# Two attention stages of an eight-stage kernel: TensorE's wait for PSUM banks, taken per score tile instead of per pair of tiles

## What is computed

```python
x = x + _L0_attn_ref(_layernorm(x), ...)   # 16 heads of 16, keys at most 128 tokens away
x = x + _L0_ffn_ref(_layernorm(x), ...)    # 8 experts, 2 chosen for each token, and a shared one
x = x + _L1_attn_ref(_layernorm(x), ...)   # 16 heads of 16, blocks of 64: neighbours, first and last block
x = x + _L1_ffn_ref(_layernorm(x), ...)    # one linear layer with weights of -1, 0 and 1
```

## Time and profile before

| | us |
|---|---|
| median of 3 runs | 2714.09 (2711.36 to 2715.87) |
| the profiled execution | 2722.96 |
| its span, first to last instruction | 2721.2 |
| TensorE busy | 2236.0 (82% of the span) |
| VectorE busy | 1889.8 (69%) |
| ScalarE busy | 1691.1 (62%) |
| GpSimd busy | 1072.8 (39%) |

### The profile page before, as it was taken

How to read it: one execution, slowest core, us unless ns; L and a number is a source line. 1 busy time by engine, 2 the same in 40 slices (tenths; PEclk the granted TensorE clock), 3 DMA queues, 4 the chain that set the end, 5 groups by cost and what they waited for, 6 DMA issues and landing times. The chain is left out here.

```text
span 2721.2 us, 71969 instructions
## 1 busy us (share of the span) xinstructions
PE 2236.0 (82%) x25421; PEld 1285.8 (47%) x25421; DVE 1889.8 (69%) x5617; ACT 1691.1 (62%) x3876; POOL 1072.8 (39%) x1325
## 2 busy tenths in 40 slices
PE   7957888888877588859999994992999999998464
PEld 4622333333324376748888883551343434343243
DVE  4538888888826577644545455765999999996285
ACT  6935777777762355514545444770788888889243
POOL 3523444444447677746666662540000000000165
PEclk9977999999988799979999997995899999999687
DMA  7442222222203266645554344763122222221296
GB/s 231 182 145 57 75 75 80 77 76 74 80 21 123 68 164 187 168 127 118 135 129 102 91 89 133 256 228 106 45 74 70 75 69 75 70 74 35 62 180 152
DMA packets 393755, 297.94 MB, mean 109 GB/s; under 512 B 258592, under 2 KB 326944, under 8 KB 393408
## 3 DMA queue, kind: packets, MB, share of 16 engines
q1 hardware_dynamic: 375904, 249.02, 34.6%
q0 software_dynamic: 12960, 35.60, 3.8%
q10 hardware_dynamic: 4544, 8.72, 1.1%
HBM read 133.53 MB, written 123.69 MB: 95 GB/s over the span
## 5 line engine op out<-in xcount | busy, mean ns | idle before, releaser
L701 ACT ACTIVATE a_pr<-a_pst 128x384 f32<-128x384 f32 (+3 forms) x2176 | 934.5, 482 | 226.4 <-PE a_pst L736 189.1
L649 DVE TENSOR_REDUCE a_mx<-a_psc 128x1 f32<-128x384 f32 (+2 forms) x1152 | 587.9, 566 | 45.3 <-PE a_psc L736 35.6
L802 PE MATMUL a_po<-a_pr,a_ve 128*17 128x128 f32 (+3 forms) x10496 | 565.3, 303 | 2.2 <-ACT a_pr L701 1.3
L644 DVE CUSTOM_DVE_ANT_0 a_cut<-a_psc,row_mask 128x384 bf16<-128x384 f32 (+1 forms) x1024 | 497.3, 522 | 88.3 <-PE a_psc L736 41.7
L736 PE MATMUL a_psc<-a_ke,a_qe 52*128 52x128 f16 (+5 forms) x3072 | 375.4, 289 | 154.3 <-DVE a_mx L644 53.5
L623 POOL TENSOR_SCALAR_AFFINE_SELECT a_pr<-a_pr 128x512 f32<-128x512 f32 x448 | 275.0, 634 | 366.7 <-ACT a_pr L701 366.7
L736 PE MATMUL a_pst<-a_qe,a_ke 53*128 53x128 f16 (+5 forms) x3072 | 368.1, 284 | 41.6 <-ACT a_pr L701 19.8
L736 PEld LDWEIGHTS a_psc<-a_ke,a_qe 52*128 52x128 f16 (+1 forms) x3072 | 123.6, 94 | 351.1 <-DVE a_mx L644 187.4
L736 PEld LDWEIGHTS a_pst<-a_qe,a_ke 53*128 53x128 f16 (+1 forms) x3072 | 113.7, 94 | 356.7 <-ACT a_pr L701 323.5
L802 PEld LDWEIGHTS a_po<-a_pr,a_ve 128*17 128x17 f32 x10496 | 194.1, 96 | 185.6 <-issue 130.5
L861 POOL MEMSET t_spread<- 128x2048 f32 x1 | 1.8, 1804 | 706.6 <-POOLq L464 706.6
(11 more groups left out here) (233 smaller groups left out, 4264.2 us busy)
## 6 DMA issues: line engine op xcount, KB each, us to landing
a_qe<-qx SPq DMA_DIRECT2D x384, 64.0 KB, 2.8
a_ke<-kx SPq DMA_DIRECT2D x384, 64.0 KB, 2.8
vx<-p_vst SPq DMA_DIRECT2D x32, 544.0 KB, 3.2
a_ve<-vx SPq DMA_DIRECT2D x64, 272.0 KB, 3.2
ox<-a_ost SPq DMA_DIRECT2D x256, 68.0 KB
qx<-p_stg SPq DMA_DIRECT2D x64, 256.0 KB, 2.8
kx<-p_stg SPq DMA_DIRECT2D x64, 256.0 KB, 3.1
x_res<-x SPq DMA_DIRECT2D x16, 512.0 KB, 9.9
```

The source lines that it names most:

```text
L644: dve.tensor_tensor_reduce(out=cut[:, n % 4, 0:width], in0=psc[(u * n_s + n) % RING][:, 0:width], in1=row_mask[:, at:at + width], scale=1. ...
L649: dve.tensor_reduce(out.unsqueeze(1), psc[(u * n_s + n) % RING][:, 0:width], AXX, ALU.max)\
L701: act.activation(pr[s % SLOTS][:, h // 2, h % 2, 0:width], pst[prob_slot(u, n) % RING][:, 0:width], ACT.Exp, scale=scale).then_inc(p_ready, 1)
L802: last = pe.matmul(po[h][32 * a:32 * a + VW, tok % CH:tok % CH + w], ve[g][:, t, a * VW:(a + 1) * VW], pr[s % SLOTS][:, a // 2, a % 2, col ...
```

## The change

Each pass of a pair now waits head by head. The matmuls of the even head wait for their own bank, and the matmuls of the odd head for theirs. The helper `products`, which interleaved the two heads piece by piece, becomes `product`, which issues all pieces of one head and then counts `ready` up. So in jobs with two pieces the order of the four matmuls changes from (head 0, piece 0), (head 1, piece 0), (head 0, piece 1), (head 1, piece 1) to (head 0, piece 0), (head 0, piece 1), (head 1, piece 0), (head 1, piece 1). Nothing else is changed: rings, jobs, the order of pairs and the other engines' programs stay.

```diff
-            def products(outs, stats, movs, pieces, ready):
+            def product(par, out, stat, mov, pieces, ready):
 
                 for k, (tok, count, col) in enumerate(pieces):
-                    for par in range(2):
-                        last = pe.matmul(outs[par][:, col:col + count], stats[par], movs[par](tok, count),
-                                         start=(k == 0), stop=(k == len(pieces) - 1),
-                                         skip_group_check=True, tile_position=(64 * par, 0))
-                        if k == len(pieces) - 1:
-                            last.then_inc(ready, 1)
+                    last = pe.matmul(out[:, col:col + count], stat, mov(tok, count), start=(k == 0),
+                                     stop=(k == len(pieces) - 1), skip_group_check=True, tile_position=(64 * par, 0))
+                last.then_inc(ready, 1)
...
-                after(pe, s_read, u * n_s + n + 1 - RING + 1)
-                products([psc[(u * n_s + n + par) % RING] for par in range(2)],
-                         [qe[g][rows(par, KS), i, t * P:(t + 1) * P] for par in range(2)],
-                         [lambda tok, count: ke[g][rows(0, KS), i, tok:tok + count],
-                          lambda tok, count: ke[g][rows(1, KS), i, tok:tok + count]], pieces, s_ready)
+                for par in range(2):
+                    after(pe, s_read, u * n_s + n + par - RING + 1)
+                    product(par, psc[(u * n_s + n + par) % RING], qe[g][rows(par, KS), i, t * P:(t + 1) * P],
+                            lambda tok, count: ke[g][rows(par, KS), i, tok:tok + count], pieces, s_ready)
...
-                free_to(pe, k + 1 - RING)
-                products([pst[(k + par) % RING] for par in range(2)],
-                         [ke[g][rows(par, KR), i, t * P:(t + 1) * P] for par in range(2)],
-                         [lambda tok, count: qe[g][rows(0, KR), i, tok:tok + count],
-                          lambda tok, count: qe[g][rows(1, KR), i, tok:tok + count]], pieces, t_ready)
+                for par in range(2):
+                    free_to(pe, k + par - RING)
+                    product(par, pst[(k + par) % RING], ke[g][rows(par, KR), i, t * P:(t + 1) * P],
+                            lambda tok, count: qe[g][rows(par, KR), i, tok:tok + count], pieces, t_ready)
```

## The result

The changed kernel takes 2624.18 us (median of 4 runs, 2622.86 to 2625.16) against 2714.98 for the kernel before; the ratio is 0.967, 95% interval 0.965 to 0.968. That is 91 us saved, where 74 were forecast. The predicted time, 2640, is 16 us too high, and the range (2610 to 2685) holds the result.

What follows compares the result with a forecast made beforehand. Bound in the masked stage: TensorE and VectorE waiting for each other in a ring. Savings 53 + 10 + 3 + 6 + 2 + 0 = 74 us took the profiled 2722.96 to 2649, median 8.9 lower: 2640; range 2610 to 2685.

Steps and rivals of the forecast that it cites:

- The ring through VectorE: Masked stage, first pass: TensorE and VectorE wait for each other, 1.18 us a period, with neither full.
- ScalarE's 44 us in the list of waits: Masked stage, second pass: weight loads' waits for ScalarE, 44.1 us of 200, claimed to be largely apparent.
- The mean of ring and path: Masked stage: new period is the mean of 1.18 (ring) and 0.89 (TensorE's own path), 1.03 us; over a unit 15.9.
- Masked stage: Unit from 18.15 to 16.35 us, saving 53 us over 29.5 units, plus 10 in the opening and 3 at the end.
- My 0.45 for ScalarE's copies and the turn: Masked unit: 0.45 us added to the mean of 15.9 for two copies of `a_po` and the turn, giving 16.35.
- The opening of two units: Masked stage, two units of first pass alone: VectorE becomes the bound, at best 11 us saved, 10 taken.
- Stage without a mask: Opening saves 6 us, end 2; steady part 0, with ends of -25 and +58 us, as gain and loss cancel.
- the new order: Stage without a mask, two-piece pairs: odd head starts 0.07 us later, paid 12 times, 0.8 us a unit.
- A: Larger gain: copies cost nothing more, stage without a mask gets half its 25 us; 100 us saved, 2614; chance 0.12.
- B: Smaller gain: second pass's added wait costs 0.06 us a pair; 27 us saved, 2687, or 2655 with half; chance 0.16.
- C: No change: the stall only moves, as if TensorE reached the pair when both banks are free; chance 0.04.
- D: Slower: heads of two-piece pairs don't overlap, odd head about 0.34 us late, 28 times a unit; 2790; chance 0.06.

Runs made afterwards that it cites:

- e1: Changed kernel with the second pass's waits and matmul order as before, so waits by head in the first pass alone: 2649.97 us, ratio 0.975.
- e2: Kernel before with the changed second pass only, so waits by head in the second pass alone: 2702.07 us, ratio 0.994.
- e6: Changed kernel with the second pass's product of head 0 done twice: 2835.54 us, one run.
- e7: Kernel before with the second pass's product of head 0 done twice: 2912.42 us, one run.
- e3: Changed kernel with the waits put back to those of the pair, so only the order of the matmuls is new: 2719.30 us, ratio 1.0005.
- e4: Kernel before with waits by head, but the pieces of the two heads interleaved as before: 2633.27 us, ratio 0.969.

## Why the prediction was right, and where it was off

*The bound.* Right. The ring through VectorE set the masked stage's period: e1 shows that its wait alone brings 1.46 of 1.65 us a unit, and e2 that the second pass's wait brings none there by itself, so that taking ScalarE's 44 us in the list of waits as largely apparent was right. The mean of ring and path is shown where it was worked out, between 192-column groups: 1.03 with the change, 1.11 with 0.17 added to the path (e6), 1.18 unmoved with 0.17 added where the ring alone binds (e7).

*Masked stage.* Forecast 53 + 10 + 3 = 66, measured 66.4. The steady units gained a tenth less than forecast: 16.49 us for 16.35. My 0.45 for ScalarE's copies and the turn was an allowance with no measurement behind it, and 0.6 is what was needed above the mean of 15.9. About half of it lies in four periods of 128-column groups near the unit's start, the turn's among them: they take 4.36 us, where the mean of the ring (1.18) and the path (0.27 + 0.35 + 0.17, and 0.28 once for the turn) gives 4.08. The opening of two units, forecast at 10 and "at best 11", gained 11.2; the other 1.5 of the table's 12.7 are a steady unit's. The end gained 2.8 more than I gave it. That the sum comes out within 1 us is luck in part, because these errors cancel. VectorE's busy share went to 93%, not 96%, and the waits for VectorE fell to 51%, not to less than half.

*Stage without a mask.* This is the step that failed: forecast 8 us, measured 24.5, which is nearly all that the total is off by. The term was the new order, costed at 0.07 us for each of 12 pairs, 0.8 a unit, so that gain and loss cancelled to 0. e3 put it at 0.02 a unit, nothing, and e4 has the new order 0.08 a unit better once the waits are by head. The reason was an assumption, that the odd head's first piece starts after the even head's second because it is written there. The rows of before, with the old order, could not show this. The lower end of this term, no cost, was the true one. The waits' gain is then what is left, 0.46 a unit, just over half of VectorE's 4.3%. Nor did I give the second pass's wait any gain, where e2 has 0.25 of it.

*The skill's rule.* In the Trainium skill, the page "TensorE: Matmul & The Clock Gate" (Part 3, the list of what overlaps) has a weight load overlap matmuls in flight only in another row group, though the same part, above that list, also allows a load into a background buffer. e3's four loads, the last two into halves whose product has just begun, start within 22 ns, so this trace goes on disagreeing with the list as it stands. The same list of the Trainium skill says that matmuls are strictly in order in start and end; in e3's pair a matmul written third starts before the one written second, so the trace does not agree as to starts.

*Rivals.* A (2614) is 10 us below the result, the forecast 16 above it. Its half for the stage without a mask was right (12 in the steady units, measured 13.5), its other half was not: copies that cost nothing would have given 67 in the masked units, measured 47.9. B is refuted. With waits by head in the second pass the masked unit is 0.2 shorter than without (16.49 for e1's 16.69), and e2's unit without a mask falls; its sign, 0.06 between the heads of a second-pass pair, isn't there in the timeline above, where both heads' loads and products start together at 419.29. C is refuted by the result, D by e3. D's time was summed wrongly, too: its 225 us come on top of the forecast's 2640, which already has the 74 taken off, so it is 2865 and not 2790.

## What to carry to other kernels

When one wait covers two banks, take it per bank, and issue all that a head needs behind its own wait: an interleaved order puts one head's work behind the other's wait. Before costing a new wait on an engine that works in order, write its period as ring and as own path; if both come near, expect about the mean where nothing else waits (over a whole masked unit about three quarters of what the mean promised came through, 1.65 of 2.25 us), and look for work to put into the gap that is left: here that was worth another 50 us. A TensorE that reads as 98% busy may still be waiting between two matmuls whose records overlap.

## What the runs showed of the hardware that was not expected

Two matmuls on different halves of TensorE's rows started within 7 ns of each other although a third, on the first one's half, stands between them in the program and started some 60 ns later (e3; in all 644 pairs counted there the one written third started first). So for TensorE it is too simple to say that an engine runs its instructions in the order in which they are written: the starts kept that order within a half of the rows only. A semaphore wait is another matter: where one stands ahead of the odd head's matmul, the even head's second piece, written behind it, waits with it (e4, 1.05 us a pair for 0.93).

The clock: in e6 and e7, the two kernels with a doubled product, TensorE stayed at a granted clock of 0.50 (1.2 GHz) from the stage's opening for 13 units after it, with TensorE busy 200.00 of 200 us in both (300 to 500 us), and then rose to full clock for the rest of the stage. The other kernels rise behind the opening (with the change, 0.50 from 200 to 220 us and 1.00 from 240 on). At that clock a unit is 27.4 us in e6 and 27.5 in e7, so with either kind of waits TensorE is the bound there. That cost an estimated 130 us in e6 (13 units at 10.0 more), more than the added work. Why it stayed low I did not find, and a single run of each doesn't say how often it happens.
